# Graph network, last node update: output bias as a rank-one product on TensorE, gate folded into the reciprocals, rectifier on 512 columns, final addition on GpSimd

## The reference, cut to what matters

```python
h = x @ node_fc_W + node_fc_b
...
h_att = segment_sum(alpha[:, None] * s_att, dst) / kk
h_rel = segment_sum(msg_rel, dst) / mm
h_red = relu(concatenate([h_att, h_rel]) @ out_fc_W + out_fc_b)
h_out = where(deg > 0, h_red, h)
gate = sigmoid(x @ gate_W + gate_b)
x = layernorm(x + gate * h_out + (1.0 - gate) * x)
```

## Time and profile before

| | us |
|---|---|
| median of 3 runs (2212.79 to 2216.94) | 2215.26 |
| profiled execution, its own time | 2217.47 |
| span of the profiled execution | 2215.7 |
| `phase_nodes1` in it, from the first product to the end of the span | 2122 to 2215.7 |
| busy in the span: PE / DVE / ACT / POOL | 1641.7 / 1319.9 / 1128.0 / 1612.1 |

### The profile page before, as it was taken

The page is one execution under the profiler, slowest core; times in us unless marked ns, Lnnn a source line. Parts: engine busy times, 40 slices in busy tenths (PEclk is TensorE's granted clock), DMA queues, the critical chain, the costliest instruction groups (busy, mean ns, idle before and its releaser), DMA issues. The chain is left out here.

```text
span 2215.7 us, 43419 instructions
## 1 busy us (share of the span) xinstructions
PE 1641.7 (74%) x9963; PEld 1000.0 (45%) x9963; DVE 1319.9 (60%) x5221; ACT 1128.0 (51%) x3319; POOL 1612.1 (73%) x1703
## 2 busy tenths in 40 slices
PE   5877777787788888944877677766777676777774
PEld 5222222222233323213646566655666565665664
DVE  4765566556554554444766666666666666665669
ACT  3434343333444444621666666555656566655548
POOL 5767777777777777777677777777777777777635
PEclk8989999999899999975989989899888999889888
DMA  8453444343434434435522222222222222222213
GB/s 277 160 184 128 130 130 130 128 150 115 145 130 136 133 122 149 151 110 113 181 67 66 66 66 66 62 65 66 61 66 65 66 60 66 66 62 65 62 57 119
DMA packets 115985, 235.06 MB, mean 106 GB/s; under 512 B 32910, under 2 KB 68231, under 8 KB 106423
## 3 DMA queue, kind: packets, MB, share of 16 engines
q0 software_dynamic: 52832, 109.39, 20.4%
q1 hardware_dynamic: 56522, 97.21, 12.0%
q10 hardware_dynamic: 6540, 27.42, 3.5%
HBM read 166.01 MB, written 67.89 MB: 106 GB/s over the span
## 5 line engine op out<-in xcount | busy, mean ns | idle before, releaser
L461 POOL DMA_INDIRECT d_region<-d_h,d_region x784 | 755.8, 964 | 248.0 <-issue 209.5
L214 POOL DMA_INDIRECT acc<-d_src_product,b_region x760 | 718.4, 945 | 251.8 <-issue 200.6
L907 DVE SCALAR_TENSOR_TENSOR banks<-banks,b_region,acc 128x128 f32<-128x128 f32 x784 | 277.1, 354 | 419.2 <-DMA acc<-d_src_product,b_region 418.6
L1683 DVE TENSOR_TENSOR acc<-acc,banks 128x160 f32 x784 | 252.3, 322 | 220.4 <-PE banks L1482 84.4
L689 PE MATMUL banks<-acc,b_region 64*128 64x512 f32 x1176 | 318.9, 649 | 35.9 <-ACT acc L795 18.4
L1448 PE MATMUL banks<-shift_ident,d_region 128*128 128x128 f32 x784 | 135.1, 297 | 249.6 <-DMA d_region<-d_h,d_region 237.9
L917 DVE SCALAR_TENSOR_TENSOR acc<-acc,b_region,banks 128x128 f32<-128x128 f32 x784 | 264.3, 337 | 0.0
L1479 PE MATMUL banks<-d_region 128*128 128x128 f32 x1568 | 247.9, 310 | 0.2 <-DVE d_region L1644 0.2
L1482 PE MATMUL banks<-d_region,pick 128*128 128x128 f32 x1568 | 241.4, 303 | 0.0
L1479 PEld LDWEIGHTS banks<-d_region 128*128 128x128 f32 x1568 | 233.4, 227 | 1.3 <-issue 0.4
L795 ACT ACTIVATE gate_col<-banks,b_region 128x1024 f32<-128x1024 f32 x147 | 158.5, 1111 | 142.0 <-PE banks L689 140.9
(11 more groups left out here) (271 smaller groups left out, 2428.3 us busy)
## 6 DMA issues: line engine op xcount, KB each, us to landing
d_runs<-acc SPq DMA_DIRECT2D x48, 1024.0 KB, 4.4
acc<-ea ACTq DMA_DIRECT2D x25, 1024.0 KB, 5.2
d_region<-d_h,d_region POOLq DMA_INDIRECT x784
d_region<-d_rel SPq DMA_DIRECT2D x49, 256.0 KB
acc<-d_src_product,b_region POOLq DMA_INDIRECT x760
hT<-xT SPq DMA_DIRECT2D x7, 448.0 KB, 7.4
d_src_product<-acc SPq DMA_DIRECT2D x7, 448.0 KB, 7.1
d_gates<-acc ACTq DMA_DIRECT2D x196, 6.0 KB
```

The costliest lines, as they stand in the source:

```text
L214: pool.indirect_dma_start(self.rows[:, s, j, :], None, table, bass.IndirectOffsetOnAxis(self.idx[:, k:k + 1], 0)).then_inc(self.gathered[s ...
L461: pool.indirect_dma_start(rows[:, s, :], None, table, bass.IndirectOffsetOnAxis(idx[:, s:s + 1], 0)).then_inc(gathered[q], 16)
L907: nc.vector.scalar_tensor_tensor(stepped[:, k % STEPS, :], wwp, wgt[:, k:k + 1], rows[:, s, j, :], ALU.mult, ALU.add).then_inc(ch, 1)
L1683: nc.vector.tensor_tensor(w, w, UZ[q % 2][:, :, j, :], ALU.add).then_inc(ad, 1)
```

## The change

It does five things, all in `phase_nodes1`.

- The bias leaves POOL. PE adds to product 0 of each block a product with one row: the sum of exponentials (one row of 128 nodes) times `ob` (L1808 of the changed kernel). `scale` then divides it away again.
- The reciprocals are multiplied once by `cu` (L1892, L1897), so the rectifier needs no factor. `cu` is computed ahead of the reciprocals now.
- `relu(c)` is one instruction of 128 x 512, in place (L1850); `r` is gone.
- `v = sA + h` moves from DVE to POOL (`add_rest`, L1783). It waits for the rectifier, for the rest of the sum and for norm(c-2), whose buffer it overwrites. `scale(c)` waits for add_rest(c-2) instead of relu(c-2).
- `scale_h` runs one chunk earlier in ACT's loop: `scale_h(n + 2)` behind `scale(n + 2)`, ahead of relu(n+1) and norm(n-1). POOL computes the rest of chunk n+2 behind add_rest(n).

```diff
         @block.gpsimd
...
-            for n in range(-2, NC4 - 1):
...
+            def rest(c):
...
+                pool.wait_ge(hl[s], 32 * (c // 3 + 1))
+                nc.gpsimd.tensor_tensor(x1[s][:, 0:z, :], x1[s][:, 0:z, :], col(cx, c, z), ALU.mult).then_inc(xm, 1)
+                pool.wait_ge(xm, c + 1)
+                pool.wait_ge(hm, c + 1)
+                nc.gpsimd.tensor_tensor(h[s][:, 0:z, :], h[s][:, 0:z, :], x1[s][:, 0:z, :], ALU.add).then_inc(mx, 1)
+
+            def add_rest(c):
+                z, _ = widths(c)
+                pool.wait_ge(rl, c + 1)
+                pool.wait_ge(mx, c + 1)
+                if c >= 2:
+                    pool.wait_ge(ln, c - 1)
+                nc.gpsimd.tensor_tensor(v[c % 2][:, 0:z, :], sA[c % 2][:, 0:z, :], h[c % 3][:, 0:z, :], ALU.add
+                                        ).then_inc(va, 1)
+
+            rest(0)
+            rest(1)
+            for n in range(NC4):
+                add_rest(n)
                 if n + 2 < NC4:
...
+                    rest(n + 2)
...
                     for k in range(K):
                         last = nc.tensor.matmul(bank_of(c, b, k), acc[:, k, blk], w[:, k * P:(k + 1) * P],
-                                                start=True, stop=True)
+                                                start=True, stop=k > 0)
+                        if k == 0:
+                            nc.tensor.matmul(bank_of(c, b, 0), acc[0:1, 4, blk], ob[0:1, :], start=False, stop=True)
...
                 if c >= 2:
-                    act.wait_ge(rl, c - 1)
+                    act.wait_ge(va, c - 1)
...
                 act.wait_ge(pm, c + 1)
-                if c >= 2:
-                    act.wait_ge(va, c - 1)
-                for k in range(z):
-                    last = nc.scalar.activation(r[c % 2][:, k, :], sA[c % 2][:, k, :], ACT.Relu,
-                                                scale=cu[:, 4 * c + k:4 * c + k + 1])
-                last.then_inc(rl, 1)
+                nc.scalar.activation(sA[c % 2][:, 0:z, :], sA[c % 2][:, 0:z, :], ACT.Relu).then_inc(rl, 1)
...
                     scale(n + 2)
+                    scale_h(n + 2)
                 if 0 <= n + 1 < NC4:
-                    scale_h(n + 1)
                     relu(n + 1)
...
+            c_.link(nc.vector.reciprocal(rz[:, 4:NBLK, :], rz[:, 4:NBLK, :]))
+            nc.vector.tensor_tensor(rz[:, 4:NBLK, :], rz[:, 4:NBLK, :],
+                                    cu[:, 4:NBLK].unsqueeze(2).to_broadcast([P, NBLK - 4, K]), ALU.mult).then_inc(zr, 1)
...
-                dve.wait_ge(bi, c + 1)
+                dve.wait_ge(sa, c + 1)
...
-                dve.wait_ge(rl, c + 1)
-                dve.wait_ge(mx, c + 1)
-                if c >= 2:
-                    dve.wait_ge(ln, c - 1)
-                nc.vector.tensor_tensor(v[c % 2][:, 0:z, :], r[c % 2][:, 0:z, :], h[c % 3][:, 0:z, :], ALU.add
-                                        ).then_inc(va, 1)
                 dve.wait_ge(va, c + 1)
```

More of the change, by code:

```diff
@@ L1712, in phase_nodes1 @@
     with ExitStack() as ctx:
-        (zt, zr, gs, cf, pr, sa, bi, pm, rl, hm, va, ask, root, sh, ln, xm, mx, st, half, ch) = new_sems(*["g_" + n for n in (
+        (zt, zr, gs, cf, pr, sa, pm, rl, hm, va, ask, root, sh, ln, xm, mx, st, half, ch) = new_sems(*["g_" + n for n in (
             "sums_turned", "sums_inverted", "gate", "coefficients", "products",
-            "scaled", "bias_added", "products_joined", "relu_done", "h_scaled", "rest_added", "root_asked",
+            "scaled", "products_joined", "relu_done", "h_scaled", "rest_added", "root_asked",
             "root_done", "shift_done", "normed", "x1_scaled", "mixed", "eps", "third_joined", "chain")])
@@ L1727, in phase_nodes1 @@
         h, x1 = ([v3(cb(G4)) for _ in range(3)] for _ in range(2))
-        sA, r, v = ([v3(ca(G4)) for _ in range(2)] for _ in range(3))
+        sA, v = ([v3(ca(G4)) for _ in range(2)] for _ in range(2))
         y = [v3(cb(G4)) for _ in range(2)]
@@ L1766, in _ @@
             pool.wait_ge(cf, 1)
-            for n in range(-2, NC4 - 1):
[L1768 to L1772, removed]
-                if n + 2 < NC4:
[L1774 to L1784, removed]
+            def rest(c):
+                z, _ = widths(c)
+                s = c % 3
+                pool.wait_ge(hl[s], 32 * (c // 3 + 1))
[4 more added lines that the diff above has]
+            def add_rest(c):
+                z, _ = widths(c)
+                pool.wait_ge(rl, c + 1)
[8 more added lines that the diff above has]
+                add_rest(n)
+                if n + 2 < NC4:
+                    rest(n + 2)
         @block.tensor
@@ L1877, in _ @@
             nc.vector.memset(eps, EPS).then_inc(st, 1)
[L1878 to L1881, removed]
             dve.wait_ge(gs, 1)
@@ L1887, in _ @@
             nc.vector.memset(stats[0][:, 0, :], 0.0).then_inc(cf, 1)
+            dve.wait_ge(zt, 1)
+            sums = [bank[n][:, 0:K * NBLK].rearrange("p (b k) -> p b k", k=K) for n in (6, 7)]
+            c_.link(nc.vector.tensor_scalar(rz[:, 0:4, :], sums[0][:, 0:4, :], 0.5, None, ALU.max))
+            c_.link(nc.vector.reciprocal(rz[:, 0:4, :], rz[:, 0:4, :]))
+            nc.vector.tensor_tensor(rz[:, 0:4, :], rz[:, 0:4, :], cu[:, 0:4].unsqueeze(2).to_broadcast([P, 4, K]), ALU.mult
+                                    ).then_inc(zr, 1)
             dve.wait_ge(zt, 2)
             c_.link(nc.vector.tensor_scalar(rz[:, 4:NBLK, :], sums[1][:, 4:NBLK, :], 0.5, None, ALU.max))
-            nc.vector.reciprocal(rz[:, 4:NBLK, :], rz[:, 4:NBLK, :]).then_inc(zr, 1)
+            c_.link(nc.vector.reciprocal(rz[:, 4:NBLK, :], rz[:, 4:NBLK, :]))
+            nc.vector.tensor_tensor(rz[:, 4:NBLK, :], rz[:, 4:NBLK, :],
+                                    cu[:, 4:NBLK].unsqueeze(2).to_broadcast([P, NBLK - 4, K]), ALU.mult).then_inc(zr, 1)
             dve.wait_ge(zr, 2)
```

## The result

The changed kernel takes **2280.18 us** (median of 4 runs, 2275.96 to 2280.95) beside 2216.1 for the kernel before on the same chip: a ratio of **1.0281**, 95% interval 1.0264 to 1.0298. The forecast was 2233.5, with a range of 2225 to 2240: the sign was right, the size was not. Of 64 us of slowdown 46 were not in the sum, and in no rival either.

The account below looks back on a forecast made before the run. The prediction took DVE to bound the last stage before, at 6.06 us per chunk, and the loads' ring after, at 7.87. Terms +16.1, +1.8 (beginning) and +0.3 (end) gave +18.2 on 2215.26: 2233.5 us, range 2225 to 2240.

Parts of the forecast that it names:

- the four one-row products per chunk at 0.24 each: PE, last stage: four more products per chunk at 0.24 us, 4.8 us per chunk in all, hidden outside the beginning.
- the list of what would show the forecast wrong: Signs against it: norms 6 us apart, scale_h idle for nothing, or PE or POOL's L1783 as scale's longest wait.
- The price for a low clock: PE: 0.34 us per full product at the low clock (5.47 / 16), and 6.7 us per chunk (5.33 x 1.25).
- the ring: Last stage: norm(c-4) to x1(c) landed 4.45, scale_h 1.17, relu 0.60, norm(c-3) 1.65; 7.87 us per chunk.
- From the stage's start to norm(0): Beginning of the last stage: eight more products and one more DVE step, partly regained; +1.8 us.
- From norm(0) to norm(8): Eight turns of 7.87 us plus 1.6 for one late load, 64.6 against 48.5 us: +16.1 us.
- From norm(8) to norm(12): End of the last stage: 12.2 us against 11.9, +0.3 us.
- The rectifier: ACT: one rectifier of 512 columns per chunk instead of four, 0.60 us to the next step, bounds 0.49 and 0.72.
- POOL's addition: POOL: add_rest costs what L1784 costs alone, 1.27 us.
- DVE's saving worth nothing: DVE loses L1915, 10.7 us on the chain, but then waits for POOL's addition instead, so nothing is gained.
- DVE stays the bound and gets faster: Rival, chance 0.04: neither ACT nor loads late, all 10.7 us of L1915 come off the chain, 2206.7 us.
- both rings: The loads' ring, 7.87 us per chunk, and norm, add_rest, scale, scale_h, relu, norm without load waits, 5.80 per chunk.

Follow-up runs that it names:

- the kernel with 128 rows: The changed kernel with the bias product on all 128 rows (bias in row 0, zeros below) instead of one row: 2241.6 us, ratio 1.0094.
- the kernel with gathered products: The changed kernel with the four one-row products of a chunk in a row at its end: 2234.5 us.
- The third buffer: The changed kernel with one-row products gathered, load(c+4) issued before the wait for norm(c), and three buffers of sA instead of two: 2213.07 us, ratio 0.9960.
- with 64 rows: The changed kernel with the bias product on 64 rows (rows 1 to 63 of its moving side zero) instead of one: 2249.77 us.

## Why the prediction was wrong, point by point

**The step that failed** is the one on PE in the part-by-part sum: the four one-row products per chunk at 0.24 each, which made 4.8 us per chunk, hidden. They were priced by their columns. What counted was their neighbours: between products on 128 rows each of them makes two changes of shape, and in this alternation the clock stayed at its lower level. The block measured 2.73 us, the chunk 10.9 (the four small products 2.9 with their changes, the sixteen full ones 8.0), and PE became the bound. No rival had PE in it, only the list of what would show the forecast wrong, so the range could not hold the time.

The price for a low clock was wrong as well. The rows of 5.33 and 5.47 us, read as sixteen products at the low clock, were at it for some six tenths of their time. The window of the first one in the kernel before (columns as above):

```profile
2174.89:2180.22 5.33, 5.33 (x32) 5.14 (x32) 5.23 (x20) 3.21 (x9) 2.74 (x2) 0.70 0.25 70
```

The granted clock is 0.70 on average, 0.50 up to 2178 and 1.00 behind that. At 0.50 throughout a full product takes 0.43, not 0.34 (the kernel with 128 rows, 2.14 / 5), and twenty take 8.6 us, not 6.7: that alone is above the ring's 7.87, so that nothing but the ring reaches 7.87 held only as long as the clock rose.

What a change of shape costs could be seen in the kernel before. An earlier stage alternates shapes on PE as well, there by columns, and its loader stands idle at each change (loader groups of the whole span, then a timeline):

```profile
L1465 PEld LDWEIGHTS banks<-d_region 128*128 128x128 f32 x392 | 63.5, 203 | 56.9 <-issue 55.4 <-DVE d_region L1665 1.5
...
L1456 PEld LDWEIGHTS banks<-d_region 128*32 128x32 f32 x1568 | 31.8, 111 | 36.8 <-issue 36.8
```

```profile
1900.72 0.16 PEld L1456 LDWEIGHTS banks<-d_region 128*32 128x32 f32 x8 [0.17 <-issue]
1901.08 0.30 PEld L1465 LDWEIGHTS banks<-d_region 128*128 128x128 f32 x2 [0.20 <-issue]
```

36.8 us of idle loader before groups of 128 x 32, released by nothing that is seen: 0.17 to 0.20 a change. Eight changes per chunk at 0.2 on top of 4.8 would have been 6.4, on top of 8.6 it would have been 10.2, above the ring's 7.87, and PE a rival. The Trainium skill, TensorEngine Tiling (Array Packing), section "Tiling Modes", says that a change of the tiling mode drains TensorE. It gives no price, and the prediction does not weigh it. If the change from 128 rows to one is such a change, which no run here shows, the trace agrees, with the 0.22 us of idle loader above. That the clock would stay low through a whole stage stood in no row of before.

**The other steps**, against the kernel with gathered products, which is the forecast kernel without that term's mistake (one profile of each). From the stage's start to norm(0): 31.2 us against 29.6, +1.5 (forecast +1.8). From norm(0) to norm(8): 63.9 against 48.5, +15.4 (forecast +16.1: six turns of 7.6 to 7.8 and two of 8.6 and 8.7, where eight of 7.87 and one late load were put). From norm(8) to norm(12): 13.35 against 13.08, +0.3 (forecast +0.3). Sum +17.3, forecast +18.2. These terms were right, and in the changed kernel they lie under PE.

**The rectifier** took 0.52 us to the next step (2162.36 to 2162.88, in the kernel without the bias) and 0.61 by its row; the forecast was 0.60, with bounds of 0.49 and 0.72. **POOL's addition** took 1.26 (forecast 1.27).

**DVE's saving worth nothing**: right as far as it went. L1915's 10.7 us are gone from the list, while the shift L1931 rose from a mean of 602 ns to 882, as it stands beside add_rest; under PE that costs nothing. The third buffer shows that the saving comes out once both rings are cut: the stage is 6.9 us shorter than before. The rival "DVE stays the bound and gets faster" said 8.6 for it; but that kernel also has other loads and one buffer more, so it does not bear the rival out.

## What to carry to other kernels

A product on TensorE is priced with its neighbours: look how many rows and columns the one ahead of it has, count the changes, and look in the loader's rows for idle time released by "issue" at such places. A rank-one product belongs at the end of a run of full ones, gathered, or on full rows with zeros. Where a step is moved ahead of others on an in-order engine, follow what its data hang on (here a load behind a norm in one queue), and move that as well, with a buffer more where the next ring closes.

## What was not expected of the hardware

- A change of the row count between neighbouring fp32 products costs 0.3 us at 1.2 GHz and 0.2 us at 2.4 GHz, with 64 rows as with one: a block took 2.73 us with either at the lower clock, and a small product with its changes 0.41 with either at the upper one (2160.94 to 2161.35 with 64 rows; 2123.55 to 2123.96 with one, at the start of the changed kernel's stage, granted clock 1.00). The loader's rows show 0.22 and 0.12 of a change as idle; PE's rows show none, and its busy time hides it.
- With one-row products between full ones TensorE was at 1.2 GHz from the second block on (the four full products at 2123.96 took 1.47 us, those at 2126.09 and ever after 2.08) and stayed there for some 138 us, though PE was busy with next to no gap. The fall is not the change's: before, the clock was 0.50 from 2124 to 2126 too, and rose within products(0). What the one-row products did was that it never rose again. With 64 or 128 rows, or with the one-row products four in a row, it came back to 2.4 GHz. With 64 rows the time between the full products was the same 0.72 us while the clock was low, so that time is not what kept it down; what about the single row does it stays open.
- The product itself costs the same with one row as with 128 (0.43 us each at 1.2 GHz). The Trainium skill, TensorE: Matmul & The Clock Gate, section "Why this matters for your kernels", says so of a single product on few rows; here the trace agrees, and the sentence alone would mislead.
